# The mask arithmetic of the second attention layer, on VectorE or on GpSimd

## The chip, the cores and the metric

The kernel is one program on 1 core of a Trainium2 chip. The metric is device time in microseconds (us) of one execution; 3 executions of the kernel before gave a median of 2976.08 us (2975.07 to 2977.13). Five engines work side by side: TensorE (PE; its weight loads are PEld), VectorE (DVE), ScalarE (ACT), GpSimd (POOL) and SyncE (SP), each with its own instruction stream in program order; they wait for one another through semaphores.

## The reference, cut to what matters

Four layers on x (8 batches x 1024 nodes x 256 features) with one matrix adj (1024 x 1024): two graph layers, then two attention layers with 8 heads of 32 features. Each layer is x = x + f(relu(layernorm(x)), adj). The two attention layers use adj differently, as a mask:

```python
# first attention layer: forbidden where adj is 0
attn = jnp.where(attn_mask[None, None] == 0, -jnp.inf, attn)
# second attention layer: an additive term for every pair
scores = scores + (1.0 - adj)[None, None, :, :] * -1000000000.0
attn = jax.nn.softmax(scores, axis=-1)
```

So the mask tensor held on the chip has other values in the second attention layer than in the first: adj has to be loaded again and turned into (adj - 1) times 1e9, up to the sign with which this kernel keeps its scores.

## The kernel before, in words

The attention phase runs 16 jobs: jobs 0 to 7 are the 8 batches of the first attention layer, jobs 8 to 15 those of the second. A job has 64 units: 8 heads times 8 tiles of 128 query rows; unit u of a job handles head u // 8 and row tile u % 8. Units are counted through a job boundary here: units 64, 65, ... of job 7 are units 0, 1, ... of job 8.

For each unit, TensorE computes 128 x 1024 scores into one of two PSUM buffers (`scores`, L720). VectorE adds the mask's row tile, keeps the row minimum, and writes the result to SBUF (`masked`, L939). ScalarE takes the exponential (`exp`, L870). TensorE transposes the result in two halves of 4 tiles (`transposes`, L732), ScalarE and VectorE copy the halves out of PSUM (L875, L1014), and TensorE multiplies by the values every second unit (`values`, L751). Between units stand blocks of projection work, by tables of fixed steps (`MID`, `NEXT`, `EARLY`). TensorE's order at step u is: scores of unit u + 2, the block of the table, values, transposes of unit u. VectorE's order at step u is: `masked` of unit u + 2, the block, the copy of a half, and here also the mask arithmetic.

Scores of a head read q and k tiles (`t_q`, `t_k`) that SP's queue gathers within the chip, 8 DMAs of 128 KB for each head (`load_head`, L635 and L636). The first head of the next job is loaded when its projections are done and 56 units of this job have their scores. TensorE waits for these 8 DMAs ahead of unit 64's scores.

The change of mask takes place at one point only, the end of job 7. The mask is 8 row tiles of 128 x 1024 f32, 512 KB each, and one semaphore per tile counts its load:

- GpSimd (`load_mask3`, L1155) issues the load of row tile t as soon as VectorE has finished `masked` of unit 56 + t, the last reader of that tile in the old mask.
- VectorE (`mask3`, L1020) waits for the load of row tile t and computes the tile in place. It does this for t = 0 to 6 at the end of steps 57 to 63, and for t = 7 at the end of step 63 also.
- VectorE's `masked` of job 8 waits until `mask3_done` has counted the row tile that it needs: unit 64 + t needs t + 1.

Since VectorE's stream is in program order, `masked` of unit 66 stands behind the arithmetic of all 8 tiles. GpSimd has nothing else to do between the last issue and its copy L1108 near step 6 of the next job (`move_v`).

Of the kernel before, what the change touches and what calls it, by code (L numbers as in the profile page):

```python
# [19 lines left out]
ALU = mybir.AluOpType  # L20
# [393 lines left out]
UNITS = 64  # L414
# [18 lines left out]
def blocks_of(first, more):  # L433

    table = sorted((EARLY if not first else []) + MID + (NEXT if more else []))
    skip = len(EARLY) if first else 0
    return {step: (skip + i, what) for i, (step, what) in enumerate(table)}


def scalar_halves(table):  # L440


    return {u for u in range(UNITS)
            if (table[u][1][0] in ("v", "norm", "out") if u in table else u % 4 == 3 and u % 16 != 7)}


def attention_phase(nc, a, x_mid, x_mid2, out, mask, shared):

    B, N, D = a["x"].shape
    NT, DC = N // P, D // P  # L450
# [8 lines left out]
    with ExitStack() as ctx:  # L459
# [3 lines left out]
        def sem(name):  # L463
            return ctx.enter_context(nc.semaphore("t_" + name))
# [91 lines left out]
        mask_in = [sem(f"mask_in{t}") for t in range(NT)]  # L556
        mask3_done = sem("mask3_done")
# [4 lines left out]
        def block_at(job, k):  # L562

            return PER_JOB * job + FIRST_BLOCKS - len(EARLY) + k
# [364 lines left out]
        def _(dve):  # L929
            def masked(job, u, layer):  # L930

                job, u = (job + 1, u - UNITS) if u >= UNITS else (job, u)
                qt = u % NT
                if layer == 1 and job == B:

                    dve.wait_ge(mask3_done, qt + 1)

                dve.wait_ge(s_done, UNITS * job + u + 1)
                nc.vector.tensor_tensor_reduce(out=T[u % RING][:], in0=s_ps[u % 2][:], in1=mask[:, qt, :],  # L939
                                               scale=1.0, scalar=3.4e38, op0=ALU.add, op1=ALU.min,  # L940
                                               accum_out=low[:, u % RING:u % RING + 1]).then_inc(t_done, 1)
# [70 lines left out]
            def copy_pt(job, u):  # L1012
                dve.wait_ge(tr_done[1], UNITS * job + u + 1)
                nc.vector.tensor_copy(pt_of(u, 1),  # L1014
                                      pt_ps[1][:].rearrange("p (k q) -> p k q", k=HT)).then_inc(pt_done[1], 1)

            def mask3(t):

                dve.wait_ge(mask_in[t], 16)
                nc.vector.tensor_scalar(mask[:, t, :], mask[:, t, :], 1.0, -1.0e9, ALU.subtract, ALU.mult)\  # L1020
                    .then_inc(mask3_done, 1)

            def ln_stats(job, t):
                if t == 0:
                    dve.wait_ge(xa_in, 16 * job)
                nc.vector.bn_stats(stats[:, t, :], xa[:, t, :]).then_inc(stat_done, 1)

            def ln_mean(job):
                dve.wait_ge(stat_done, 8 * job)
                for t in range(NT):  # L1030
                    last = nc.vector.bn_aggr(mv[:, t, :], stats[:, t, :])
                last.then_inc(mv_done, 1)
# [21 lines left out]
            def body(job, layer, before, after):  # L1054
                table = blocks_of(before is None, after is not None)
                for u in range(UNITS):
                    if u + 2 < UNITS or after is not None:
                        masked(job, u + 2, layer if u + 2 < UNITS else after)
                    copy_first = u in table and table[u][1][0] in SHORT
                    if copy_first and u not in scalar_halves(table):  # L1060
                        copy_pt(job, u)
                    if u in table:
                        k, what = table[u]
                        early, in_next = (u, what) in EARLY, (u, what) in NEXT
                        finish_block(block_at(job, k), what, before if early else after if in_next else layer,
                                     job - 1 if early else job + 1 if in_next else job)
                    if not copy_first and u not in scalar_halves(table):
                        copy_pt(job, u)
                    if after is not None:
                        if LN_STEP <= u < LN_STEP + NT:  # L1070
                            ln_stats(job + 1, u - LN_STEP)
                        if u == LN_STEP + NT:
                            ln_mean(job + 1)
                    if layer != after and after is not None and u >= UNITS - NT + 1:
                        mask3(u - (UNITS - NT + 1))
                        if u == UNITS - 1:
                            mask3(NT - 1)

            jobs(body)
            for k, what in enumerate(LAST):  # L1080
                finish_block(tail_block(k), what, 1, JOBS - 1, k, True)
# [3 lines left out]
        def _(pool):  # L1085
# [53 lines left out]
            def norm(job):  # L1139

                pool.wait_ge(ln_chain, 2 * job)
                for p in range(NT // 2):
# [5 lines left out]
                                            rstd[:, tiles].rearrange("p (t o) -> p t o", o=1).to_broadcast([P, 2, D]),  # L1148
                                            op=ALU.mult).then_inc(hn_done, 1)

            def load_mask3():

                for t in range(NT):
                    pool.wait_ge(t_done, UNITS * (B - 1) + UNITS - NT + t + 1)
                    pool.dma_start(mask[:, t, :], a["adj"][t * P:(t + 1) * P, :]).then_inc(mask_in[t], 16)  # L1155


            for b in range(2):
# [2 lines left out]
            def body(job, layer, before, after):  # L1161
                move_v(job)
                if before is not None:
                    for p in range(XE):
                        bias_xe(job - 1, before, p)
                    if before == 0:
                        add_ln(job - 1, 0)
                        add_ln(job - 1, 1)
                    bias_xe(job - 1, before, XE)
                if after is not None:  # L1170
                    row_scale(job + 1)
                    norm(job + 1)
                if before == 0:
                    add_ln(job - 1, 2)
                    add_ln(job - 1, 3)
                if layer != after and after is not None:
                    load_mask3()
# [39 lines left out]
```

## Time and profile before

| | |
|---|---|
| median of 3 executions | 2976.08 us |
| the profiled execution, whole / span of the engines' work | 2974.42 us / 2972.6 us |
| busy: PE, DVE, ACT, POOL | 98%, 81%, 72%, 20% |
| granted TensorE clock, mean | 0.994 of full speed |
| mask loads on GpSimd's queue | 8 x 512 KB, median 10.5 us from issue to landing |
| VectorE's mask arithmetic L1020 | 8 instructions, 1715.5 to 1739.1 us |

Times are microseconds from the start of the span. In a row of a timeline the first number is the start, the second the duration, and the bracket gives the idle time of that engine ahead of the row and what ended it. A row of an issued DMA has the duration of the issue, not that of the transfer. Granted clock 1.00 is 2.4 GHz, 0.50 is 1.2 GHz. Matmul ends are modelled, so neighbouring rows of PE overlap a little.

### The profile page before, as it was taken

The numbers are of one execution on the slowest core, as the hardware profiler recorded it, in microseconds if no ns is written. First come the engines' busy times: TensorE is split into PE (matmuls) and PEld (weight loads), VectorE is DVE, ScalarE is ACT, GpSimd is POOL, SyncE is SP. The second block draws the span as 40 slices with busy tenths as digits, with TensorE's granted clock in tenths as the row PEclk, the third lists the DMA queues.
The fourth block names the chain that finished last, engine by engine and source line by source line (L and its number), as shares of the span: only waits on it lengthen the run. The fifth ranks groups of instructions, "written<-read, shape, count | busy, mean of one in ns | idle before, by whom it ended". The sixth has DMA issues, their size and how long they took to land.

```text
span 2972.6 us, 59755 instructions
## 1 busy us (share of the span) xinstructions
PE 2906.1 (98%) x23872; PEld 2199.0 (74%) x23872; DVE 2401.1 (81%) x4427; ACT 2126.1 (72%) x3794; POOL 591.3 (20%) x538
## 2 busy tenths in 40 slices
PE   7999997999999999999999989999999999999998
PEld 6888886777777777777777767777777777777776
DVE  6776775879888888888888878888888787878786
ACT  3000002888888888888888878888888888888887
POOL 2222220105050504131322323010101010101000
PEclk9999998999999999999999999999999999999999
DMA  3001003323233233232323252323233332323232
GB/s 124 29 29 58 29 29 94 70 56 90 69 83 75 71 74 83 65 93 61 96 51 97 67 140 68 90 66 85 65 81 74 82 76 72 87 55 93 65 75 58
DMA packets 123588, 217.19 MB, mean 73 GB/s; under 512 B 20016, under 2 KB 88240, under 8 KB 123312
## 3 DMA queue, kind: packets, MB, share of 16 engines
q1 hardware_dynamic: 122160, 209.14, 28.4%
q0 software_dynamic: 1152, 4.19, 0.6%
q8 instruction: 195, 3.19, 0.4%
q14 instruction: 81, 0.66, 0.1%
HBM read 53.87 MB, written 25.17 MB: 27 GB/s over the span
## 4 chain that ended last, share of the span: by engine, by line
PE 79%; ACT 2%; DVE 1%; DMA 1%; issue 0%; ACTq 0%; DVEq 0%
PE t_pt_ps L732 32%; PE t_ot_ps L751 17%; PE t_s_ps L720 15%; PE t_g_ps L705 4%; PE t_g_ps L706 4%; PE t_g_ps L707 4%; PE t_g_ps L772 1%; PE t_g_ps L776 1%; PE t_g_ps L791 1%; ACT t_T L870 1%; ACT t_PT L875 1%; DMA mask<-in_adj 1%; DVE t_st_lo L957 0%; ACT t_st_hi L860 0%; ACT t_ot L881 0%
## 5 line engine op out<-in xcount | busy, mean ns | idle before, releaser
L939 DVE CUSTOM_DVE_ANT_0 t_T<-t_s_ps,mask 128x1024 f32<-128x1024 f32 x1024 | 1240.6, 1215 | 117.3 <-PE t_s_ps L720 112.5
L870 ACT ACTIVATE t_T<-t_T,t_low 128x1024 f32<-128x1024 f32 x1024 | 1178.8, 1151 | 43.1 <-DVE t_low L939 37.9
L732 PEld LDWEIGHTS t_pt_ps<-t_ident,t_T 128*128 128x128 f32 x8192 | 885.2, 141 | 325.7 <-issue 279.5
L732 PE MATMUL t_pt_ps<-t_ident,t_T 128*128 128x128 f32 x8192 | 1112.6, 279 | 6.3 <-DVE t_PT L1014 4.5
L875 ACT ACTIVATE t_PT<-t_pt_ps 128x512 f32<-128x512 f32 x1324 | 755.9, 596 | 317.9 <-PE t_pt_ps L732 306.7
L720 PE MATMUL t_s_ps<-t_k,t_q 128*128 128x512 f32 x2048 | 729.7, 437 | 8.3 <-DMA t_k<-t_st_lo 7.1
L1014 DVE COPY t_PT<-t_pt_ps 128x512 f32<-128x512 f32 x724 | 499.1, 689 | 196.6 <-PE t_pt_ps L732 194.0
L751 PE MATMUL t_ot_ps<-t_PT,shared 128*32 128x256 f32 x8192 | 549.4, 386 | 8.1 <-ACT t_PT L875 7.9
L751 PEld LDWEIGHTS t_ot_ps<-t_PT,shared 128*32 128x32 f32 x8192 | 215.1, 109 | 255.4 <-issue 128.0
L247 ACT ACTIVATE g_yT_hi<-g_ps 128x512 fp32r<-128x512 f32 x64 | 38.3, 598 | 400.5 <-PE g_ps L187 400.5
L720 PEld LDWEIGHTS t_s_ps<-t_k,t_q 128*128 128x128 f32 x2048 | 310.6, 192 | 9.3 <-DMA t_k<-t_st_lo 7.6
L1108 POOL COPY shared<-shared 128x1024 f32<-128x1024 f32 x16 | 17.0, 1062 | 1263.8 <-PE t_ot_ps L751 1254.0
L185 PE MATMUL g_ps<-g_adjT_hi,g_h_hi 128*128 128x512 f32 x512 | 200.8, 392 | 7.2 <-DVE g_spare L362 5.6
L870 ACT ACTIVATION_READ_ACCUMULATOR t_T<-t_T,t_low 128x1 f32 x1024 | 200.6, 196 | 0.0
L186 PE MATMUL g_ps<-g_adjT_lo,g_h_hi 128*128 128x512 f32 x512 | 200.3, 391 | 0.0
L187 PE MATMUL g_ps<-g_adjT_hi,g_h_lo 128*128 128x512 f32 x512 | 199.9, 390 | 0.0
L957 DVE SCALAR_TENSOR_TENSOR t_st_lo<-t_g_ps,t_b_qk,t_st_hi 128x512 fp32r<-128x512 f32 x125 | 93.8, 750 | 66.1 <-ACT t_st_hi L860 65.1
L860 ACT ACTIVATE t_st_hi<-t_g_ps,t_b_qk 128x512 fp32r<-128x512 f32 x125 | 85.9, 687 | 42.9 <-PE t_g_ps L707 42.9
L185 PEld LDWEIGHTS g_ps<-g_adjT_hi,g_h_hi 128*128 128x128 f32 x512 | 96.7, 189 | 26.8 <-DVE g_spare L362 5.8
L187 PEld LDWEIGHTS g_ps<-g_adjT_hi,g_h_lo 128*128 128x128 f32 x512 | 96.6, 189 | 20.1
L186 PEld LDWEIGHTS g_ps<-g_adjT_lo,g_h_hi 128*128 128x128 f32 x512 | 96.7, 189 | 19.0
L705 PE MATMUL t_g_ps<-t_hT_hi,t_w_hi 128*128 128x512 f32 x250 | 100.7, 403 | 7.6 <-DVE t_st_lo L957 4.8
(185 smaller groups left out, 3158.1 us busy)
## 6 DMA issues: line engine op xcount, KB each, us to landing
t_q<-t_st_hi SPq DMA_DIRECT2D x256, 128.0 KB, 2.3
t_k<-t_st_hi SPq DMA_DIRECT2D x256, 128.0 KB, 2.4
t_k<-t_st_lo SPq DMA_DIRECT2D x256, 128.0 KB, 2.4
t_q<-t_st_lo SPq DMA_DIRECT2D x256, 128.0 KB, 2.4
shared<-x_after_graph_layers SPq DMA_DIRECT2D x8, 1024.0 KB, 6.5
t_xe<-x_after_graph_layers SPq DMA_DIRECT2D x32, 256.0 KB, 3.1
x_after_layer<-t_xe SPq DMA_DIRECT2D x32, 256.0 KB, 2.1
shared<-x_after_layer SPq DMA_DIRECT2D x8, 1024.0 KB, 6.8
```

Of the source, the lines that this page charges most:

```text
L185: mm(out, s_hi, m_hi, start=first, stop=False)
L186: mm(out, s_hi, m_lo, start=False, stop=False)
L187: return mm(out, s_lo, m_hi, start=False, stop=final)
L705: mm(dst, s_hi, m_hi, start=first, stop=False)
L706: mm(dst, s_hi, m_lo, start=False, stop=False)
L720: last = mm(s_ps[u % 2][:, cols], q4[h % 2][:, qt * P:(qt + 1) * P], k4[h % 2][:, cols], start=True, stop=True)
L732: last = nc.tensor.transpose(pt_ps[half][:, i * P:(i + 1) * P], T[u % RING][:, kt * P:(kt + 1) * P], ident[:])
L751: last = mm(ot_ps[j * HD:(j + 1) * HD, h % 2 * 2 * P:(h % 2 + 1) * 2 * P], v_sb[:, kt, h * HD:(h + 1) * HD], probs, start=kt == 0, stop=kt ...
L870: nc.scalar.activation(T[u % RING][:], T[u % RING][:], ACT.Exp, bias=low[:, u % RING:u % RING + 1], scale=-1.0, accum_out=rsum[:, u:u + 1] ...
L875: copy(pt_of(u, half), pt_ps[half][:].rearrange("p (k q) -> p k q", k=HT), ACT.Copy).then_inc(pt_done[half], 1)
L939: nc.vector.tensor_tensor_reduce(out=T[u % RING][:], in0=s_ps[u % 2][:], in1=mask[:, qt, :], scale=1.0, scalar=3.4e38, op0=ALU.add, op1=AL ...
L1014: nc.vector.tensor_copy(pt_of(u, 1), pt_ps[1][:].rearrange("p (k q) -> p k q", k=HT)).then_inc(pt_done[1], 1)
```

## The change

The mask arithmetic moves to GpSimd, into the loop that issues the loads. After the issue of load t (from t = 2 on) GpSimd waits for load t - 2 and computes tile t - 2; after the loop it computes tiles 6 and 7. VectorE no longer has any step of it; its waits of `masked` on `mask3_done` are as before.

```diff
@@ block.vector
-            def mask3(t):
-
-                dve.wait_ge(mask_in[t], 16)
-                nc.vector.tensor_scalar(mask[:, t, :], mask[:, t, :], 1.0, -1.0e9, ALU.subtract, ALU.mult)\
-                    .then_inc(mask3_done, 1)
-
...
-                    if layer != after and after is not None and u >= UNITS - NT + 1:
-                        mask3(u - (UNITS - NT + 1))
-                        if u == UNITS - 1:
-                            mask3(NT - 1)
@@ block.gpsimd
+            def mask3(t):
+
+                pool.wait_ge(mask_in[t], 16)
+                nc.gpsimd.tensor_scalar(mask[:, t, :], mask[:, t, :], 1.0, -1.0e9, ALU.subtract, ALU.mult)\
+                    .then_inc(mask3_done, 1)
+
             def load_mask3():
 
                 for t in range(NT):
                     pool.wait_ge(t_done, UNITS * (B - 1) + UNITS - NT + t + 1)
                     pool.dma_start(mask[:, t, :], a["adj"][t * P:(t + 1) * P, :]).then_inc(mask_in[t], 16)
+                    if t >= 2:
+                        mask3(t - 2)
+                for t in range(NT - 2, NT):
+                    mask3(t)
```

## Rows read from the trace of the kernel before

**Rows 1.** Timeline of GpSimd: its one copy per job, jobs 6, 7 and 8

```profile
1433.77 1.04 POOL L1108 COPY shared<-shared 128x1024 f32<-128x1024 f32 x1 [80.80 <-PE t_ot_ps L751]
1586.93 1.04 POOL L1108 COPY shared<-shared 128x1024 f32<-128x1024 f32 x1 [80.79 <-PE t_ot_ps L751]
1753.87 1.04 POOL L1108 COPY shared<-shared 128x1024 f32<-128x1024 f32 x1 [24.61 <-PE t_ot_ps L751]
```

**Rows 2.** Chain that ended last, 1690 to 1780 us: start, duration, what

```profile
1715.23 10.85 DMA mask<-in_adj
1726.10 0.69 DVE mask L1020
...
1728.23 10.87 DMA mask<-in_adj
```

**Rows 3.** Timeline of PE around the end of job 7

```profile
1727.29 1.22 PE L720 MATMUL t_s_ps<-t_k,t_q 128*128 128x512 f32 x2 [4.36 <-DMA t_k<-t_st_lo]
...
1736.66 0.63 PE L732 MATMUL t_pt_ps<-t_ident,t_T 128*128 128x128 f32 x4
1741.62 1.11 PE L732 MATMUL t_pt_ps<-t_ident,t_T 128*128 128x128 f32 x4 [4.33 <-DVE t_PT L1014]
...
1746.61 0.71 PE L720 MATMUL t_s_ps<-t_k,t_q 128*128 128x512 f32 x2
```

**Rows 4.** Timeline of PE around the end of job 6, same units

```profile
1569.30 0.71 PE L720 MATMUL t_s_ps<-t_k,t_q 128*128 128x512 f32 x2
...
1576.33 1.10 PE L732 MATMUL t_pt_ps<-t_ident,t_T 128*128 128x128 f32 x8
...
1579.68 0.71 PE L720 MATMUL t_s_ps<-t_k,t_q 128*128 128x512 f32 x2
```

**Rows 5.** Windows of 5 us: busy of each engine, granted clock, DMA share

```profile
1730.00:1735.00 5.00, 5.00 (x40) 3.76 (x36) 2.72 (x6) 3.02 (x6) 0.00 (x0) 0.74 1.06 215
1735.00:1740.00 5.00, 2.29 (x22) 1.55 (x14) 1.57 (x3) 1.51 (x3) 0.00 (x0) 0.94 0.88 235
1740.00:1745.00 5.00, 3.38 (x22) 1.84 (x22) 4.62 (x8) 2.97 (x5) 0.00 (x0) 0.50 0.01 2
```

**Rows 6.** SP's last DMA for the head of unit 64: its issue; landings of L636 there

```profile
1717.47 0.61 SPq L636 DMA_DIRECT2D t_k<-t_st_lo  x1
...
DMA to landing us min/median/max: 5.9/6.8/9.8
```

**Rows 7.** DMA issues in groups: one of four kinds of head DMA, median us to landing

```profile
t_k<-t_st_lo SPq DMA_DIRECT2D x256, 128.0 KB, 2.4
```

**Rows 8.** Timeline of DVE: mask arithmetic of row tiles 2, 3, 4, 6, 7

```profile
1719.55 0.69 DVE L1020 TENSOR_SCALAR mask<-mask 128x1024 f32<-128x1024 f32 x1
...
1726.10 0.69 DVE L1020 TENSOR_SCALAR mask<-mask 128x1024 f32<-128x1024 f32 x1 [3.84 <-DMA mask<-in_adj]
...
1728.46 0.68 DVE L1020 TENSOR_SCALAR mask<-mask 128x1024 f32<-128x1024 f32 x1
...
1735.46 0.69 DVE L1020 TENSOR_SCALAR mask<-mask 128x1024 f32<-128x1024 f32 x1 [0.71 <-DMA mask<-in_adj]
1739.12 0.69 DVE L1020 TENSOR_SCALAR mask<-mask 128x1024 f32<-128x1024 f32 x1 [2.96 <-DMA mask<-in_adj]
```

**Rows 9.** Groups by line: what GpSimd's whole-tile operations take

```profile
L1108 POOL COPY shared<-shared 128x1024 f32<-128x1024 f32 x16 | 17.0, 1062 | 1263.8 <-PE t_ot_ps L751 1254.0 <-DVE shared L967 9.8
...
L280 POOL TENSOR_TENSOR g_x<-g_x,g_bias 128x2048 f32<-128x2048 f32 x8 | 41.0, 5121 | 22.3 <-DVE g_hn L314 22.3
```

**Rows 10.** Timeline of GpSimd: issues of loads 2, 6 and 7

```profile
1711.67 0.54 POOL L1155 DMA_DIRECT2D mask<-in_adj  x1 [1.18 <-DVE t_low L939]
...
1721.67 0.54 POOL L1155 DMA_DIRECT2D mask<-in_adj  x1 [1.21 <-DVE t_low L939]
1728.23 1.03 POOL L1155 DMA_DIRECT2D mask<-in_adj  x1 [6.03 <-DVE t_low L939]
```

**Rows 11.** Timeline of DVE, end of job 6: `masked` of unit 71

```profile
1584.50 1.21 DVE L939 CUSTOM_DVE_ANT_0 t_T<-t_s_ps,mask 128x1024 f32<-128x1024 f32 x1
```

## The prediction

> **What bounds the kernel now.** The change touches one place in the run, so I priced that place first. GpSimd's copy L1108 comes once per job at a fixed step, which makes it a clock of the jobs [rows 1]: from job 6 to job 7 it takes 1586.93 - 1433.77 = 153.16 us, from job 7 to job 8, over the change of mask, 1753.87 - 1586.93 = 166.94 us. The boundary costs 13.8 us more than an ordinary one. That is all that any change to the mask work there can win, 0.46% of the run.
>
> Next, where these 13.8 us arise. The chain of waits passes through two mask loads of 10.85 and 10.87 us [rows 2]. PE's timeline has two idle stretches there. The first, 4.36 us, ends at 1727.29 with scores of unit 64, and its releaser is a DMA of `t_k` [rows 3]. The second, 4.33 us, ends at 1741.62 in the middle of a pair of transposes, unit 65, released by a VectorE copy [rows 3]. I lay job 6's end, shifted by 153.2, beside this [rows 4]:
>
> - unit 64's scores: 1727.29 - (1569.30 + 153.2) = 4.8 us late;
> - transposes of unit 65, just ahead of the second stall: 1736.66 - (1576.33 + 153.2) = 7.1 us late;
> - scores of unit 69, after it: 1746.61 - (1579.68 + 153.2) = 13.7 us late.
>
> So the first stall costs 7.1 us and the second 13.8 - 7.1 = 6.6 us (7.13 and 13.75 unrounded), idle time and slower matmuls together. The slow part shows in the windows: the granted clock averages 0.74 in 1730 to 1735, with PE busy throughout, and is 0.50 in 1740 to 1745 [rows 5], so PE goes at the lower level for some us after each idle stretch: about 2.3 us of each price.
>
> What ends each stall? The first is a transfer: the last head DMA is issued at 1717.47 and lands 9.8 us later, 1727.27 [rows 6], against a usual 2.4 us [rows 7]. The mask loads share the DMA engines with it, and the DMA share is near 1 [rows 5]. VectorE also sat 3.84 us in front of tile 3 until 1726.10 [rows 8], but TensorE does not need that result before unit 64's scores: it stands in the shadow of the head load. The second stall is VectorE's own: at step 63 it waits 0.71 us for tile 6 and 2.96 us for tile 7, and only after 1739.12 + 0.69 comes to `masked` of unit 66 and the copy for which PE waits [rows 3, 8]. Unit 66 needs row tile 2 alone, ready since about 1720.2 [rows 8]. That is a wait by program order, not by data.
>
> **The change, part by part.**
>
> Removed from VectorE: 8 tensor_scalar of 0.69 us [rows 8], 5.5 us in all. I count them at nothing by themselves: before the first stall they cannot matter, as its end is a DMA's landing, and the later ones lie beside PE's busy stretch or inside the second stall, priced below. If that cover were gone they would be worth their 5.5 us at most.
>
> Removed from VectorE: the waits for loads 3, 6 and 7. The one for load 3 is hidden by the head load, zero. Those for 6 and 7 are the second stall. With them gone VectorE does `masked` of unit 66 as soon as scores and row tile 2 are there. Gain 6.6 us, if no tile is late for its own unit.
>
> Added on GpSimd: 8 tensor_scalar of 128x1024. The trace has no such form on GpSimd. The nearest from below is the copy of the same shape, 1.06 us; from above half a two-input operation of 128x2048, 5.12 / 2 = 2.6 us [rows 9]. I take 1.1, the copy's, since this too reads one tensor, and keep 2.6 for the range. GpSimd has nothing else to do until L1108 at 1753.87, so the work costs nothing unless a tile or a load is late.
>
> The Trainium skill, "GPSIMD Engine Reference", section "Engine selection", speaks against the move: it sends elementwise work on a tile to VectorE and calls GpSimd about 2x slower for two inputs, with one input roughly at line rate. Its 2.6 cycles per element at 1.2 GHz would be an estimated 2.2 us for the tile. By that the sum would be the same, since 2.2 lies within the bounds above.
>
> Moved, GpSimd's issues: each wait for a landing now stands ahead of the later issues. Through this queue, with P for the duration of one tensor_scalar:
> - load 2 is issued at 1711.67 as before, then tile 0 is computed; load 3 as before at 1715.23, since 1712.2 + P is earlier even for 2.6 [rows 2, 10].
> - Load 5 comes after tile 2, which had landed by 1719.55 [rows 8]: at 1721 to 1722, one or two us later than now.
> - Load 6 comes after tile 3, landed 1726.08: at 1726.1 + P, that is 1727.2 (1728.7), against 1721.67 now [rows 10].
> - Load 7 comes after tile 4, landed at the latest by 1728.46 [rows 8]: at about 1729.5 (1732) against 1728.23.
>
> Do tiles come late? Unit 64 + t needs tile t. If only the first stall stays, VectorE reaches unit 71 at 1584.50 + 153.2 + 7.1 = 1744.8 [rows 11] and unit 70 some 2.5 us before. Bounds for landing 7: the DMA engines have the same bytes to move and are about full till 1739 [rows 5], so the last mask load lands near the present 1739.1, at 1739 to 1741; tile 7 is done at 1740 to 1743.6, 1.2 to 5 us ahead of its unit. Tiles 3 to 6 have more room: unit 67 is due at about 1736.9, tile 3 done at 1728.7 at the latest.
>
> The first stall stays: the head's 8 DMAs are issued as before, and loads 2, 3 and 4 are in GpSimd's queue before 1727 in both kernels. Its price could change by parts of a us either way; I take zero.
>
> **The sum.** Profiled execution: 2974.42 - 6.6 = 2967.8. The median of the runs before is 2976.08, 1.66 above the profiled one; I carry that over: 2976.08 - 6.6 = 2969.5 us, 0.22% less.
>
> **The rivals.**
>
> A, the forecast: the second stall goes, the first stays, 2969.5; chance 0.72. Its own range is 2967.5 to 2971, as the slower-clock part of a stall (2.3 here) can be about 1 more or less in another execution.
>
> B, a tile becomes late: the wait moves from VectorE's program order to tile 7. For it: load 6 took 1735.46 - 1721.67 = 13.8 us to land [rows 8, 10]; if load 7 took as long from 1732 and P were 2.6, tile 7 would be done at 1748.4, 3.6 us late; with some 1.6 for the clock that is 5.2 of the 6.6 given back: 2974.7. Against it: that 13.8 was time in a queue behind three other loads, and now only one or two are ahead. Chance 0.12.
>
> C, slower: GpSimd's in-order chain is too long. From tile 3's landing at 1726.1 five operations and two issues (0.54 to 1.03 each [rows 10]) lie before tile 7 is done: 1728 + 5P. It costs more than the old second stall once tile 7 is later than 1744.8 + 6.6 = 1751.4, thus from P = 4.7 us. At P = 5.1, the longest duration of any row here [rows 9], tile 7 is done at 1753.5, 2.1 past that point: 2978.2. Against it: that row has twice the elements and a second input. Chance 0.07.
>
> D, the first stall goes too: loads 5 and 6 come later, and the head DMAs get through. The Trainium skill, "DMA: Bandwidth & Descriptors", section on queues, rings and completion order, has each DMA engine go round-robin between the queues with work. By that rule the head gains only if GpSimd's queue runs empty before 1727. With the usual 2.4 us the head would land at 1719.9 and the whole 13.8 could go; but unit 71 would then be due at 1737.7, and tile 7, ready at 1740.2 at the earliest, takes back 2.5: 2976.1 - 13.8 + 2.5 = 2964.8. Against it: loads 3 and 4 are queued until 1726 and after, whatever becomes of 5 and 6. Chance 0.05.
>
> E, nothing comes of it: something else holds PE at the place of the second stall, as the DMAs of the next head. They are not due before unit 72. Time 2976; chance 0.04.
>
> **How the numbers follow.** About 0.2% (6 us) is what a measurement of this kernel can tell from no change, and the forecast gain is just over it, so A is split: 0.58 of its 0.72 above the line, 0.14 below. Faster: 0.58 + 0.05 (D) = 0.63. Same: 0.14 + B 0.12 + E 0.04 = 0.30. Slower: C 0.07. The range of 8 in 10 takes A whole and parts of B and D: 2966.0 to 2974.0.
>
> **What would show it.** After: the period of L1108 over the boundary about 160.3 instead of 166.9; one PE idle stretch of about 4.4 us ended by a DMA of `t_k` at about 1727, no second; one stretch at the low clock instead of two; GpSimd's tensor_scalar near 1.1 us; issues of loads 6 and 7 at about 1727 and 1730; no wait of L939 for the mask. Wrong it would be by a `masked` waiting for GpSimd, by P above 4 us, or by another length of the first stall.

## The result and the profile after

Over 20 runs each the kernel before takes 2974.98 us (median; the three first runs, on which the prediction stood, had 2976.08) and the changed one 2971.64 us (2967.43 to 2977.21). The ratio is 0.9986, with a 95% interval of 0.9979 to 0.9992: 0.14% less, some 4.2 us (2.4 to 6.2) where 6.6 were forecast; the two medians by themselves lie 3.3 us apart. The predicted 2969.5 us is 2.1 below the measured median, which lies inside the range of 2966.0 to 2974.0 but outside the 2967.5 to 2971 that the forecast rival A had as its own. The gain is real, but under the 0.2% line for which I had given the most chance.

| | before | changed |
|---|---|---|
| median of 20 | 2974.98 us | 2971.64 us |
| profiled execution, span | 2972.6 us | 2969.9 us |
| busy DVE, POOL | 2401.1, 591.3 us | 2396.5, 619.5 us |
| two job periods across the boundary, less 2 x 153.2 | 13.7 us | 9.7 us |

The last row is the measure used from here on and called the boundary's cost: from the copy on GpSimd in job 7 to the one in job 9, less two ordinary periods. In the changed kernel the copy has line L1098; timeline of GpSimd, jobs 7, 8 and 9:

```profile
1586.69 1.04 POOL L1098 COPY shared<-shared 128x1024 f32<-128x1024 f32 x1 [80.77 <-PE t_ot_ps L751]
...
1749.17 1.04 POOL L1098 COPY shared<-shared 128x1024 f32<-128x1024 f32 x1 [1.70 <-PE t_ot_ps L751]
```

The period over the boundary is 162.48 us, against 1753.87 - 1586.93 = 166.94 in [rows 1], and the next, to 1902.78, is 153.61, still 0.4 too long. 162.48 + 153.61 - 306.4 = 9.69. Before: 166.94 and then 153.20 give 13.74. The difference, 4.05, lies inside the interval of the ratio.

Timeline of GpSimd in the changed kernel, the issues L1151 and the arithmetic L1144 that moved there:

```profile
1711.37 0.54 POOL L1151 DMA_DIRECT2D mask<-in_adj  x1 [1.18 <-DVE t_low L939]
1711.97 3.66 POOL L1144 TENSOR_SCALAR mask<-mask 128x1024 f32<-128x1024 f32 x1
1715.70 0.60 POOL L1151 DMA_DIRECT2D mask<-in_adj  x1
...
1720.74 3.62 POOL L1144 TENSOR_SCALAR mask<-mask 128x1024 f32<-128x1024 f32 x1
1724.42 0.60 POOL L1151 DMA_DIRECT2D mask<-in_adj  x1
1725.73 3.62 POOL L1144 TENSOR_SCALAR mask<-mask 128x1024 f32<-128x1024 f32 x1 [0.71 <-DMA mask<-in_adj]
1729.42 0.60 POOL L1151 DMA_DIRECT2D mask<-in_adj  x1
...
1733.78 0.60 POOL L1151 DMA_DIRECT2D mask<-in_adj  x1
1736.42 11.04 POOL L1144 TENSOR_SCALAR mask<-mask 128x1024 f32<-128x1024 f32 x3 [2.04 <-DMA mask<-in_adj]
```

One operation takes 3.62 us, not 1.1. The eight lie within 3.62 to 3.66 us, beside a busy VectorE and beside an idle one, and `masked` takes 1.22 us on VectorE as before, so the two engines did not slow each other here. Loads 5, 6 and 7 go out at 1724.42, 1729.42 and 1733.78; [rows 10] has loads 6 and 7 at 1721.67 and 1728.23. The last three operations run without a break from 1736.42 to 1747.5, merged here into one row.

Timeline of VectorE, `masked` of units 69, 70 and 71:

```profile
1740.08 1.22 DVE L939 CUSTOM_DVE_ANT_0 t_T<-t_s_ps,mask 128x1024 f32<-128x1024 f32 x1 [1.12 <-POOL mask L1144]
...
1743.79 1.23 DVE L939 CUSTOM_DVE_ANT_0 t_T<-t_s_ps,mask 128x1024 f32<-128x1024 f32 x1 [2.48 <-POOL mask L1144]
...
1747.50 1.23 DVE L939 CUSTOM_DVE_ANT_0 t_T<-t_s_ps,mask 128x1024 f32<-128x1024 f32 x1 [1.88 <-POOL mask L1144]
```

The waits for loads of [rows 8] are gone, and three waits for GpSimd, 5.5 us together, have come instead, one tile after another.

Timeline of PE, the rows that answer to [rows 3]: the first stall, unit 66's scores, the late transposes, and the first matmuls after these:

```profile
1726.23 1.22 PE L720 MATMUL t_s_ps<-t_k,t_q 128*128 128x512 f32 x2 [3.74 <-DMA t_k<-t_st_lo]
...
1731.53 0.70 PE L720 MATMUL t_s_ps<-t_k,t_q 128*128 128x512 f32 x2
...
1745.68 0.66 PE L732 MATMUL t_pt_ps<-t_ident,t_T 128*128 128x128 f32 x4 [1.84 <-DVE t_PT L1014]
1746.10 1.03 PE L720 MATMUL t_s_ps<-t_k,t_q 128*128 128x512 f32 x2
```

No stop is as long as 4.33 us at the place of the second stall any more. PE stops in small pieces between 1742 and 1746 instead, and is late again. To split the cost, unit 66's scores serve: they come after the first stall and ahead of what followed. An ordinary boundary has them 13.7 us before the copy of job 7, shifted by 153.2. Here they are 1731.53 - (1586.69 - 13.7 + 153.2) = 5.3 us late: the first stall's price, 7.1 before. The other 4.4 us of 9.7 come from tiles 5 to 7; the second stall's price was 6.6.

The windows show where the first stall is cheaper here. Columns as in [rows 5]; the granted clock is third from the end of each row:

```profile
1725.00:1730.00 5.00, 3.77 (x25) 1.85 (x26) 1.23 (x2) 0.06 (x1) 4.23 (x3) 0.66 1.02 169
1730.00:1735.00 5.00, 5.00 (x45) 3.41 (x43) 3.72 (x7) 4.87 (x9) 4.24 (x3) 1.00 1.04 222
1740.00:1745.00 5.00, 3.27 (x31) 1.96 (x30) 2.44 (x5) 2.27 (x5) 4.84 (x3) 1.00 0.04 13
1745.00:1750.00 5.00, 4.32 (x29) 2.39 (x30) 3.12 (x7) 2.95 (x6) 3.30 (x2) 0.66 0.00 0
```

In 1730 to 1735 the clock is at the upper level, where [rows 5] has a mean of 0.74. PE had been idle for 3.74 us rather than 4.36, and the lower level ended sooner. After the waits for the late tiles it falls again, to a mean of 0.66 in 1745 to 1750.

### The profile page after: what moved, and what is told of

It reads as the page before. It is cut to its first block, busy times and chain, and to the rows that moved or that the text cites. A ratio compares the mean times of both kernels' runs of the same rounds, so it can differ in the third digit from the quotient of the medians.

```text
span 2969.9 us, 59755 instructions
## 1 busy us (share of the span) xinstructions
PE 2906.6 (98%) x23872; PEld 2198.5 (74%) x23872; DVE 2396.5 (81%) x4419; ACT 2126.9 (72%) x3794; POOL 619.5 (21%) x546
## 4 chain that ended last, share of the span: by engine, by line
PE 79%; ACT 2%; DVE 1%; POOL 1%; DMA 0%; issue 0%; ACTq 0%; DVEq 0%
PE t_pt_ps L732 32%; PE t_ot_ps L751 17%; PE t_s_ps L720 15%; PE t_g_ps L705 4%; PE t_g_ps L706 4%; PE t_g_ps L707 4%; PE t_g_ps L772 1%; PE t_g_ps L776 1%; ACT t_T L870 1%; PE t_g_ps L791 1%; ACT t_PT L875 1%; POOL mask L1144 1%; DMA mask<-in_adj 0%; DVE t_st_lo L957 0%; ACT t_st_hi L860 0%; ACT t_ot L881 0%
## 5 line engine op out<-in xcount | busy, mean ns | idle before, releaser
L1098 POOL COPY shared<-shared 128x1024 f32<-128x1024 f32 x16 | 17.0, 1063 | 1240.5 <-PE t_ot_ps L751 1230.9
```

## The experiments

All ratios are to the kernel before, run on the same chip in the same session, with a 95% interval. "First" is the lateness of unit 66's scores, the first stall's price; "rest" is the remainder of the boundary's cost. (In e6 a new wait falls ahead of unit 66, so the two can't be parted there. e4 has a single execution and so no ratio.)

| kernel | ratio | cost | first | rest |
|---|---|---|---|---|
| before | | 13.7 | 7.1 | 6.6 |
| changed | 0.9986 (0.9979 to 0.9992) | 9.7 | 5.3 | 4.4 |
| changed again (e0) | 0.9989 (0.9980 to 0.9998) | 10.1 | 6.4 | 3.7 |
| e1 short operation | 0.9981 (0.9972 to 0.9990) | 7.2 | 7.2 | 0 |
| e2 loads first | 1.0005 (0.9996 to 1.0014) | 15.6 | 7.3 | 8.3 |
| e3 VectorE late | 0.9984 (0.9975 to 0.9993) | 10.7 | 8.5 | 2.2 |
| e4 forms | | 7.3 | 7.4 | 0 |
| e5 head first, from tile 3 | 0.9961 (0.9947 to 0.9975) | 4.1 | 2.0 | 2.1 |
| e6 head first only | 1.0005 (0.9996 to 1.0014) | 12.1 | | |
| e7 no mask change | 0.9954 (0.9941 to 0.9968) | 0.0 | 0 | 0 |
| e8 head first, from tile 2 | 0.9957 (0.9943 to 0.9971) | 2.2 | 0.1 | 2.1 |
| e9 second operation | 1.0007 (0.9998 to 1.0017) | 16.0 | 7.5 | 8.5 |
| e10 two on GpSimd | 0.9962 (0.9948 to 0.9976) | 1.7 | 0.0 | 1.7 |
| e12 all on GpSimd, other form | 0.9960 (0.9947 to 0.9974) | 1.2 | 0.0 | 1.2 |

Costs come from one profile each, and 1 us is 0.034% of the run. The interval of a ratio covers several us, so the costs separate what the ratios cannot: the time of the profiled execution less its cost runs from 2960.7 to 2965.4 us over the 14 profiles, a spread that arises outside the boundary. How far the cost itself varies from one execution to the next is known from two profiles of the changed kernel only, 9.7 and 10.1 with parts that differ by up to 1.1, so differences of 1 us and less between costs are not read here.

My theory after the result, S: moving the arithmetic did end VectorE's wait by program order, as forecast, and an operation that takes 3.62 us on GpSimd, eight times in order, put late tiles in its place. The main rival, R: the waits for landings between the issues make the last loads late, whatever the operation takes.

### e1: GpSimd's operation made short

```diff
-                nc.gpsimd.tensor_scalar(mask[:, t, :], mask[:, t, :], 1.0, -1.0e9, ALU.subtract, ALU.mult)\
+                nc.gpsimd.tensor_scalar(mask[:, t, 0:16], mask[:, t, 0:16], 1.0, -1.0e9, ALU.subtract, ALU.mult)\
```

> The changed kernel with GpSimd's mask arithmetic cut to 16 of the 1024 columns of each tile (the other columns stay unconverted: part of the mask's computation is left out); all waits, loads and their order are kept. The boundary between jobs 7 and 8, beyond an ordinary job, costs 13.8 us in the kernel before and 9.3 in the changed one. Theory S (the duration of GpSimd's operation, 3.62 us, keeps the rest of the second stall): the operation falls to about 0.3 us, no masked step waits for GpSimd, and only the first stall is left: boundary cost 5 to 7 us, run 7 to 8.5 us faster than before. Rival R (the waits for landings between the issues make the last loads late, whatever the operation takes): loads 6 and 7 still go out only after tiles 3 and 4 landed, near 1726 and 1728, and a masked step waits for a late tile: boundary cost 8 to 9 us.

Measured: 2970.24 us, ratio 0.9981, boundary's cost 7.2 us, all of it ahead of unit 66. GpSimd's timeline, tiles 3, 4 and 5:

```profile
1725.00 0.27 POOL L1144 TENSOR_SCALAR mask<-mask 128x16 f32<-128x16 f32 x1 [4.47 <-DMA mask<-in_adj]
1725.33 0.60 POOL L1151 DMA_DIRECT2D mask<-in_adj  x1
1728.28 0.27 POOL L1144 TENSOR_SCALAR mask<-mask 128x16 f32<-128x16 f32 x1 [2.35 <-DMA mask<-in_adj]
1728.61 0.60 POOL L1151 DMA_DIRECT2D mask<-in_adj  x1
1732.67 0.27 POOL L1144 TENSOR_SCALAR mask<-mask 128x16 f32<-128x16 f32 x1 [3.46 <-DMA mask<-in_adj]
```

GpSimd still waits for landings in front of its issues (loads 6 and 7 at 1725.33 and 1728.61), and no `masked` waits for a tile. S holds and R falls; with a short operation the forecast of this document comes true, second stall 0, first stall unchanged. The profile agrees to 0.1 us; the ratio's interval (3 to 8 us gained) holds the 6.6 too. The expectation, a cost of 5 to 7 us and a gain of 7 to 8.5, was a little too good, since I had counted on the cheaper first stall of the changed kernel's profile.

### e2: all loads issued ahead of the arithmetic

```diff
                     pool.dma_start(mask[:, t, :], a["adj"][t * P:(t + 1) * P, :]).then_inc(mask_in[t], 16)
-                    if t >= 2:
-                        mask3(t - 2)
-                for t in range(NT - 2, NT):
+                for t in range(NT):
                     mask3(t)
```

> The changed kernel with all 8 loads issued first and GpSimd's 8 operations after them. Theory S: the loads go out as early as before or earlier, but the chain of 8 operations of 3.62 us starts only near 1723.5, tile 2 is ready near 1734.4 and tile 7 near 1752.5, against needs near 1732 and 1743: boundary cost 14 to 16 us, no better than the kernel before. Rival R (late issues are what costs): the loads land earlier, and the boundary cost falls below the changed kernel's 9.3 us.

Measured: 2977.72 us, ratio 1.0005, cost 15.6 us. Waits for the mask, in total, times, longest:

```profile
DVE t_T L939 <- POOL mask L1144: 10.3, 6, 2.5
```

Loads 5 to 7 went out 5 to 11 us earlier than in the changed kernel (the last three at 1718.94, 1720.25 and 1723.18) and the time got worse, by 5.9 us of boundary's cost. GpSimd's eight operations ran from 1723.79 to 1753.43, 29.64 us in one piece, and six units waited. In this kernel the interleaving of issues and arithmetic is worth more than early loads; R is refuted from the other side.

### e3: the arithmetic stays on VectorE, later

```diff
                 if layer == 1 and job == B:
+                    if u < NT:
+                        mask3(qt)
                     dve.wait_ge(mask3_done, qt + 1)
...
-                    if layer != after and after is not None and u >= UNITS - NT + 1:
-                        mask3(u - (UNITS - NT + 1))
-                        if u == UNITS - 1:
-                            mask3(NT - 1)
```

> The kernel before with VectorE's arithmetic of row tile t moved to just ahead of masked of unit 64 + t; GpSimd issues the loads only. If the second stall was VectorE's program order and nothing else, it goes here too, at 0.69 us per tile: boundary cost 6 to 8 us (the first stall, 5.4 to 7.1, and up to 1 for the added work), run 6 to 7.5 us faster than before. Rival (the work itself has to leave VectorE): 8 x 0.69 = 5.5 us come onto the path of a pace of 2 us per unit, boundary cost 11 to 13 us.

Measured: 2971.91 us, ratio 0.9984, cost 10.7 us. The time is as for the changed kernel; the cost falls between the two expectations, for a reason that neither named. The rest, with the 5.5 us of work on VectorE, is only 2.2 us, so the second stall was the place of the work in the order, not the engine. But the first stall became longer:

```profile
1730.45 1.22 PE L720 MATMUL t_s_ps<-t_k,t_q 128*128 128x512 f32 x2 [6.24 <-DMA t_k<-t_st_lo]
```

6.24 us of idle time, and 8.5 of lateness, in the one profile. The DMAs of L636 for this head took up to 11.1 us to land, against 9.8 in [rows 6] and 9.2 in the changed kernel. Its mask loads are free to go out early, at 1720.60, 1721.91 and 1724.83 for 5, 6 and 7, which could be the reason; but e2 issued its loads at the same distances and had 4.84 us of idle time. What made this stall longer is open; see e0.

### e7: no change of mask at all

```diff
-                    dve.wait_ge(mask3_done, qt + 1)
+                    pass
...
-                if layer != after and after is not None:
-                    load_mask3()
```

VectorE's `mask3` steps are taken out as well.

> The kernel before without the change of mask: no loads, no arithmetic, the second attention layer uses the first one's mask (part of the computation is left out). If both stalls come from the mask's loads and arithmetic, the boundary costs 0 to 0.5 us more than an ordinary job and the run is 13.5 us faster than before (0.45%). Rival (the head's slow landing, which ends the first stall, has another cause, such as the change of weights at that place): a stall on t_k near 1727 remains, boundary cost 3 to 7 us.

Measured: 2961.20 us, ratio 0.9954, cost 0.0 (two periods of 153.20 and 153.19). Both stalls, the one on `t_k` too, are the mask's doing. 13.7 us is therefore all that could be had, and the ratio says the same (3.2 to 5.9 thousandths; 13.7 us are 4.6).

### e4: what the operation takes, by form

```diff
+                col, s1, s2, o1, o2 = [(1024, 1.0, None, ALU.subtract, None), (1024, -1.0e9, None, ALU.mult, None),
+                                       (1024, 1.0, -1.0e9, ALU.subtract, ALU.mult), (1024, -1.0e9, 1.0e9, ALU.mult, ALU.add),
...
+                                       (512, 1.0, None, ALU.subtract, None), (256, 1.0, None, ALU.subtract, None)][t]
```

> The changed kernel with another form of GpSimd's tensor_scalar on each row tile, to price the operation (the mask values come out partly wrong, part of the computation is left out): tile 0 one subtraction on 1024 columns, 1 one multiplication on 1024, 2 subtraction and multiplication on 1024 as in the change, 3 multiplication and addition on 1024, 4 and 5 subtraction and multiplication on 512 and 256, 6 and 7 one subtraction on 512 and 256. If the time is per element and per arithmetic step, the one-step forms take about 1.9 us on 1024 columns, the two-step ones 3.6, and 512 columns half of each. Rival (this instruction goes through slower code whatever the steps): all forms on 1024 columns take about 3.6 us.

Timeline of GpSimd. L1148 is the two-step form, of tiles 2 to 5; L1149 the one-step form, here of tiles 0 and 1:

```profile
1712.52 2.80 POOL L1149 TENSOR_SCALAR mask<-mask 128x1024 f32<-128x1024 f32 x1
...
1716.18 2.78 POOL L1149 TENSOR_SCALAR mask<-mask 128x1024 f32<-128x1024 f32 x1
...
1719.83 3.64 POOL L1148 TENSOR_SCALAR mask<-mask 128x1024 f32<-128x1024 f32 x1 [0.32 <-DMA mask<-in_adj]
...
1725.92 1.03 POOL L1148 TENSOR_SCALAR mask<-mask 128x1024 f32<-128x1024 f32 x1 [1.79 <-DMA mask<-in_adj]
...
1730.32 1.91 POOL L1148 TENSOR_SCALAR mask<-mask 128x512 f32<-128x512 f32 x1 [2.81 <-DMA mask<-in_adj]
```

The kernel ran once, in 2968.21 us. Neither expectation holds. Subtraction or multiplication alone takes 2.8 us, subtraction then multiplication 3.64, and multiplication then addition 1.03, as fast as GpSimd's copy of that shape. 512 columns of the slow form take 1.91, so it goes by the element: (3.64 - 1.91) / 512 = 3.4 ns each. The row at 1725.92 is a single case of its form; e9 and e12 repeat it.

### e9: a second operation per tile

```diff
+                nc.gpsimd.tensor_scalar(mask[:, t, :], mask[:, t, :], 1.0, 0.0, ALU.mult, ALU.add)\
+                    .then_inc(mask_x, 1)
+                pool.wait_ge(mask_x, t + 1)
                 nc.gpsimd.tensor_scalar(mask[:, t, :], mask[:, t, :], 1.0, -1.0e9, ALU.subtract, ALU.mult)\
```

> The changed kernel with a second GpSimd operation of the same form ahead of each mask operation (times 1, plus 0), so 7.25 us per tile instead of 3.62. If GpSimd's in-order chain sets the end, tile 7 is ready 8 operations and 6 issues after 1712, near 1774, 26 us later than in the changed kernel: boundary cost 33 to 38 us, run 24 to 28 us slower than the changed kernel. Rival (the waits for landings fill the gaps, and the operations lie in their shadow): boundary cost below 20 us.

The expectation was wrong in its price: the added operation is multiplication and addition and took 1.05 us, so a tile costs 4.8 us instead of 7.25. Groups by line:

```profile
L1148 POOL TENSOR_SCALAR mask<-mask 128x1024 f32<-128x1024 f32 x8 | 29.1, 3635 | 0.7
L1145 POOL TENSOR_SCALAR mask<-mask 128x1024 f32<-128x1024 f32 x8 | 8.4, 1054 | 0.4
```

The mechanism shows all the same. Tile 7 is ready at 1754.5 instead of 1747.5, and the boundary's cost rises from 9.7 to 16.0 us. Of these 6.3 us, 4.1 are in the rest, where the late tiles count; 2.2 are in the first stall's price, which varies without the change too (see e0). With some 1.2 us more on each tile the kernel lost its whole gain: 2977.49 us, ratio 1.0007.

### e5, e6 and e8: the head's DMAs first

For e5 and e8 the arithmetic is placed as in e3, for e6 as in the kernel before. One wait is added:

```diff
                     pool.wait_ge(t_done, UNITS * (B - 1) + UNITS - NT + t + 1)
+                    if t == 3:
+                        pool.wait_ge(head_in[0], 128 * (4 * B + 1))
                     pool.dma_start(mask[:, t, :], a["adj"][t * P:(t + 1) * P, :]).then_inc(mask_in[t], 16)
```

e8 has `t == 2` there.

> VectorE's arithmetic just ahead of its unit (as in the run before with that placing), and GpSimd's mask loads from tile 3 on wait until the head of unit 64 has landed. Theory: the first stall is the head's 8 DMAs sharing the DMA engines with loads 2 to 4 and what follows; with those held back the head lands 2 to 4 us after its last issue, near 1720, the first stall goes, and unit 71 needs its tile near 1738 while the last load lands near 1738 to 1740: boundary cost 1 to 4 us, run 10 to 13 us faster than before (2963 to 2966). Rival (the DMA engines are full anyway, and the bytes only move): the stall reappears at a tile of units 67 to 71, boundary cost 7 us or more.

> The kernel before with only the holding back of loads 3 to 7 until the head of unit 64 has landed. VectorE's arithmetic stands at steps 57 to 63 as before. If the end of the second stall is set by the last load's landing near 1739, wherever TensorE waits before it, then the first stall's time reappears in the second: boundary cost 11 to 14 us, no gain or little. Rival (the two stalls are separate prices that add up): the boundary cost falls by the first stall's 7 us, to about 7.

> As the run that held the loads back from tile 3 on, but from tile 2 on. There the head's last DMA of its 8 still landed 6 to 7 us after issue, though loads 3 to 7 were held: load 2, issued 0.3 us ahead of the head's first DMA, is the only other transfer near. Theory: load 2 alone slows the head; held too, the head lands 2 to 4 us after its last issue, near 1721, TensorE does not wait for it, and loads 2 to 7 start some 4 us earlier than there: boundary cost 1.5 to 3.5 us instead of 4.1, run about 12 us faster than before. Rival (the head's DMAs are slow at that place for another reason): the wait of about 1.7 us for t_k stays, boundary cost about 4 or, as one more load is late, 5.

e5: 2965.24 us, ratio 0.9961, cost 4.1 us, just above the 1 to 4 expected. Its first stall is still there, 1.74 us long, because the head's last DMA took 7.1 us to land even so:

```profile
1725.27 0.73 PE L720 MATMUL t_s_ps<-t_k,t_q 128*128 128x512 f32 x2 [1.74 <-DMA t_k<-t_st_lo]
```

e8 holds load 2 back too, the one that goes out just ahead of the head's DMAs. Then the landings of `t_k` there are as anywhere else in the run ([rows 7]), and the loads start near 1719.5 instead of 1725.8:

```profile
DMA to landing us min/median/max: 2.4/2.4/2.4
```

TensorE does not wait for `t_k`, and the cost is 2.2 us: 2963.32 us, ratio 0.9957. Load 2 is issued 1.1 us ahead of the head's first DMA (not 0.3, as the expectation has it). So one 512 KB load was enough to slow the head from 2.4 to 6 or 7 us, and with the loads behind it the slowest landing was 9.2 to 11.1 us in the kernels that hold nothing back. The Trainium skill, "DMA: Bandwidth & Descriptors", section on queues, rings and completion order, has each DMA engine alternate between the queues that have work; a head that shares the engines with a load, and is fast alone, fits that.

e6 shows why the two prices in my sum do not simply add. It removes nearly all of the first stall (0.8 us left) and gains almost nothing: 2976.63 us, ratio 1.0005, cost 12.1 us, as expected. Waits of VectorE's arithmetic, in total, times, longest:

```profile
DVE mask L1020 <- DMA mask<-in_adj: 10.1, 4, 6.7
```

VectorE's fixed order now waits 10.1 us for loads, where [rows 8] has 7.5, with 6.7 us at tile 3. While the arithmetic stands at steps 57 to 63, VectorE can't pass the loads, and time saved ahead of it comes back there.

### e10 and e12: the work shared, and the fast form

e10 is e8 with tiles 0 and 1 on GpSimd, in the time in which it waits for the head. e12 is the changed kernel with the fast form and with the loads held back:

```diff
-                nc.gpsimd.tensor_scalar(mask[:, t, :], mask[:, t, :], 1.0, -1.0e9, ALU.subtract, ALU.mult)\
+                nc.gpsimd.tensor_scalar(mask[:, t, :], mask[:, t, :], -1.0e9, 1.0e9, ALU.mult, ALU.add)\
...
+                    if t == 2:
+                        pool.wait_ge(head_in[0], 128 * (4 * B + 1))
                     pool.dma_start(mask[:, t, :], a["adj"][t * P:(t + 1) * P, :]).then_inc(mask_in[t], 16)
-                    if t >= 2:
-                        mask3(t - 2)
-                for t in range(NT - 2, NT):
+                    if t == 1:
+                        mask3(0)
+                        mask3(1)
+                for t in range(2, NT):
                     mask3(t)
```

> Loads from tile 2 on held back until the head of unit 64 has landed; GpSimd computes row tiles 0 and 1 in the time that it waits anyway, VectorE tiles 2 to 7 just ahead of their units. The late placing on VectorE cost about 0.4 us per two units (a pair of units took 4.36 us instead of 3.93). Two tiles less should give 0.4 us back: boundary cost 0.4 us below that of the same kernel with all 8 on VectorE, 1 to 3 us. Rival: GpSimd's two operations of 3.62 us, ready near 1721, push the loads back by about 1 us and a later tile becomes late: boundary cost equal or higher.

> The arithmetic of all 8 tiles on GpSimd, as in the change, but written as a multiplication by -1e9 and then an addition of 1e9, the form that took 1.03 us on 1024 columns in the run on forms (3.62 us as subtraction and multiplication); tiles 0 and 1 before, tiles 2 to 7 behind the issues, and loads from tile 2 on held back until the head of unit 64 has landed. If the order of the two steps alone makes the operation slow, it takes 1.03 to 1.06 us here on every tile. The kernel with the same holding back and the arithmetic on VectorE has a boundary cost of 2.2 us, of which the late placing on VectorE is some 1.6. Without it 0.5 to 1.5 us should be left, or up to 2 if tile 7, landing near 1737.8 there, is 1 to 2 us late for its unit near 1737.3: run 12 to 13.5 us faster than before. Rival (1.03 us was due to something else in that run, as the tile being the only one of its form): the operation takes 2.8 us or more, tiles 5 to 7 are late, boundary cost 5 us or more.

e10: 2965.00 us, ratio 0.9962, cost 1.7 us, 0.5 below e8's where 0.4 were expected, though single profiles do not separate so little. e12: 2964.84 us, ratio 0.9960, cost 1.2 us. Its operations:

```profile
L1144 POOL TENSOR_SCALAR mask<-mask 128x1024 f32<-128x1024 f32 x8 | 8.4, 1048 | 11.5 <-DMA mask<-in_adj 11.5
```

1.05 us on all eight tiles: the form of the two steps was the price of the operation. The slow form and the fast one differ in the steps (subtraction or addition) as well as in their order, and no run parts these two. What is left is a wait of `masked` of 2.5 us for the last two tiles, at their landing. By their profiles e12 has the lowest cost and e8 the lowest median; their intervals overlap widely, and the timings don't rank e5, e8, e10 and e12. All four beat both kernels of this case; by the ratios they are 11 to 13 us faster than the kernel before.

### e0: the changed kernel once more

> The changed kernel once more, beside the others on one chip. If the first stall's length follows from the order of the loads, it is 3.5 to 4.2 us of idle time again and the boundary cost 9 to 10 us; if its shortening was chance, it may be 4.4 us or more and the cost 10 to 11.

Measured: 2972.39 us, ratio 0.9989, cost 10.1 us, with 4.58 us of idle time and a price of 6.4 in the first stall, where the first profile had 3.74 and 5.3. Both figures lie in the range of the second expectation, that the shortening was chance, and outside the first. Over the eight profiles in which nothing was held back for the head, the price ran from 5.3 to 8.5. The loads' order does not explain it: the two profiles of the changed kernel are the lowest, but e9, with its loads held back by GpSimd's arithmetic even longer, has 7.5, and e2 and e3, alike in their loads, have 7.3 and 8.5. Two profiles of one kernel differ by 1.1 us. Even so the second profile's price is still 0.7 below that of the kernel before. So I can't say whether the 1.8 us by which the first stall was cheaper in the changed kernel's profile belongs to the change or to chance.

## Why the prediction was right or wrong, by its own steps

**The ceiling of 13.8 us** was right: e7 leaves none of it.

**The first stall is the head's transfer sharing the DMA engines with the mask loads**: right, by e8. That VectorE's wait for tile 3 lies in its shadow is right too, by e1 and e3, where VectorE no longer waits for tile 3 and the stall is as long or longer. "Its price could change by parts of a us" was too narrow: -1.8 and -0.7 in two profiles of the changed kernel, +1.4 in e3. The prediction's "about 2.3 us of each price" for the slower clock holds for the second stall (6.6 - 4.33); for the first it is 2.8 (7.13 - 4.36).

**The second stall is program order, worth 6.6 us**: right. e1 has exactly the first stall left. e3 gets the same with the work still on VectorE, for 2.2 us, so the count of nothing for the 5.5 us of removed work was too low where they are placed late, and fair for the change.

**The operation on GpSimd: 1.1, at most 2.6 us.** This is the term of the sum that failed: it took 3.62. Both bounds were of other operations, a copy and a two-input addition, and the one-input operation lay above both. I had taken the two-input form as the worst case because it reads more. e4 shows that reads are not what counts here: with the same tile, one input and two scalar steps it is 1.03 or 3.64 us by which steps stand in which order. The Trainium skill, "GPSIMD Engine Reference", section "Engine selection", has one-input operations roughly at line rate. The copy and the multiplication with addition agree with that (1.04 and 1.05 us), the operation of this change does not. The 2.6 cycles per element behind the prediction's estimate of 2.2 us stand in the Trainium skill, "GPSIMD Engine Reference", section "Elementwise — side-by-side cycle accounting", as the floor for two inputs. So they were no measure of this operation, and 3.62 us lies above the 2.2 too.

**Tiles are in time.** This step failed, and it rested on that term. With 3.62 us rival C's chain, 1728 + 5P, puts tile 7 at 1746.1; measured was 1747.5, for a need at 1584.5 + 153.2 + 5.3 = 1743.0. The chain in detail was load 5, 11.92 us from issue at 1724.42 to landing, and then three operations in a row. So the outcome is A's mechanism with B's wait in it: -6.6 from the second stall, +4.4 from late tiles, and -1.8 from the first stall, together -4.0. Of the prediction's signs of being wrong two came: a `masked` that waits for GpSimd, and another length of the first stall. The third, P above 4 us, did not.

**Rival C, its break-even at P = 4.7 us**: e9 tests it, with 4.8 us per tile. The boundary costs 2.2 us more there than in the kernel before, and the ratio is 1.0007 (0.9998 to 1.0017). The point is in about the right place, if anything below 4.7: on a straight line between 9.7 us at P = 3.62 and 16.0 at 4.8 the old cost of 13.7 is reached at an estimated 4.4. The change as made is about 1 us per operation from being worthless.

**The carry-over to the median**: I had started from three runs with 2976.08; over 20 it is 2974.98. That took 1.1 us of the difference back, so that the time came out nearer to the forecast than the gain. With the late tiles alone the forecast would have been 2969.5 + 4.4 = 2973.9, at the edge of the range. The cheaper first stall and the lower median, neither of them foreseen, brought the time down to 2971.64: that it lies well inside the range is in part luck.

**Rival D**, the head getting through because loads are later, happened in small part at most, if at all (see e0). Made on purpose, in e8, it was worth more than the whole change.

## What to carry to other kernels

When an in-order engine waits for data that its next instructions don't need, the stall is a matter of order: moving the work to an idle engine and moving it later on the same engine both remove it, and the second needs no new price. An operation moved to another engine must be priced there in its own form; a bound from other operations, even heavier looking ones, is none. Before counting two stalls as two prices, ask whether the engine behind the second would only wait longer once the first is gone, and look for a small, urgent transfer that starts just behind a large one.

## What the runs showed of the hardware

GpSimd's tensor_scalar on 128x1024 f32 took 3.62 us as subtraction then multiplication, 2.8 us as either alone, and 1.03 to 1.06 us as multiplication then addition (17 operations in e4, e9 and e12; the single steps twice, in e4). With the addition behind it the multiplication was thus faster than alone.

A single 512 KB load on GpSimd's queue, issued 1.1 us ahead of eight gathers of 128 KB on SP's queue, took their landings from 2.3 to 2.4 us (e8) to 5.5 to 7.1 us (e5).

The first stall was followed by some us at the lower clock level, and what that cost differed between profiles: lateness less idle time came to 1.6 us in the changed kernel (5.3 - 3.74), 1.8 in its second profile (6.4 - 4.58), 2.7 in the kernel before (7.1 - 4.36).
